# Two graph layers on one core: fp16 products for the whole of layer 1's sum, a mask made by an adding transfer, and a new order

## What is computed

```
h  = x @ W;   e = leaky_relu(h @ a_src + (h @ a_dst)^T)            # 4096 x 4096
valid = adj > 0 and the column's h.sum != 0
att = softmax(where(valid, e, NEG));  att = att where att >= 1e-4, else 0
x1 = layernorm(x + elu(h + (att * valid.sum(axis=1)) @ h))          # layer 0
s  = leaky_relu(x1 @ ks^T), masked by adj > 0, softmax over rows
out = layernorm(x1 + softmax(s) @ ks)                               # layer 1
```

## Time and profile before

| what | value |
|---|---|
| median of 3 runs | 885.51 us (885.41 to 885.6) |
| the profiled execution | 886.26 us, its span 884.4 us |
| TensorE busy | 849.4 us, 96% of the span |
| VectorE busy | 783.3 us, 89% |
| ScalarE busy | 763.8 us, 86% |
| GpSimd busy | 231.0 us, 26% |
| transfers | 43.93 MB counted, mean 50 GB/s |

### The profile page before, as it was taken

One profiled execution on the slowest core, in us unless ns is written; L12 is line 12 of the kernel. 1 busy time (PEld: TensorE's weight loads), 2 busy tenths in 40 slices (PEclk: granted clock), 3 DMA queues, 4 the chain that ended last, 5 costly groups with the idle time before them and its releaser, 6 DMA issues.

```text
span 884.4 us, 17581 instructions
## 1 busy us (share of the span) xinstructions
PE 849.4 (96%) x7111; PEld 732.9 (83%) x7111; DVE 783.3 (89%) x955; ACT 763.8 (86%) x747; POOL 231.0 (26%) x428
## 2 busy tenths in 40 slices
PE   7479999999999999999999999999999999999995
PEld 4376788899888888988888889888888998888885
DVE  1789999999999999999999999999999999998744
ACT  4588988889998888899988888999888889998753
POOL 1431143321223333212233331122333312222200
PEclk9898999999999999999999999999999999999999
DMA  9832222122222211222222112222221122200000
GB/s 236 124 67 50 52 49 41 28 43 55 54 55 54 55 34 30 47 54 55 54 54 54 28 32 53 54 55 54 55 52 24 34 55 54 55 7 7 4 4 10
DMA packets 23408, 43.93 MB, mean 50 GB/s; under 512 B 5024, under 2 KB 18464, under 8 KB 19232
## 3 DMA queue, kind: packets, MB, share of 16 engines
q0 software_dynamic: 7696, 34.34, 21.5%
q1 hardware_dynamic: 15200, 8.39, 3.7%
q10 hardware_dynamic: 432, 0.07, 0.1%
HBM read 75.04 MB, written 2.10 MB: 87 GB/s over the span
## 4 chain that ended last, share of the span: by engine, by line
PE 90%; DVE 3%; DMA 2%; POOL 2%; issue 2%; ACT 1%; POOLq 0%; SPq 0%; DVEq 0%; ACTq 0%
PE bank L336 25%; PE work L234 24%; PE bank L364 10%; PE bank L368 6%; PE work L313 6%; PE work L318 6%; PE work L314 6%; PE bank L365 5%; DMA adj_sb<-adj 1%; DMA att<-x 1%; POOL row L870 0%; POOL edges L879 0%; PE bank L374 0%; DVE att1T L690 0%; ACT att L460 0%
## 5 line engine op out<-in xcount | busy, mean ns | idle before, releaser
L234 PE MATMUL work<-ident,att 128*128 128x128 f32 x2080 | 245.9, 274 | 11.9 <-DMA att<-x 6.0
L234 PEld LDWEIGHTS work<-ident,att 128*128 128x128 f32 x2080 | 232.5, 141 | 19.3 <-issue 9.2
L336 PE MATMUL bank<-h_all,att0T 128*128 128x128 f32 x2048 | 239.1, 275 | 0.0
L336 PEld LDWEIGHTS bank<-h_all,att0T 128*128 128x128 f32 x2048 | 233.7, 192 | 0.0
L500 ACT ACTIVATE att1T<-work 128x1024 f16<-128x1024 f32 (+1 forms) x128 | 125.5, 1048 | 34.7 <-PE work L234 34.7
L640 DVE SCALAR_TENSOR_TENSOR att<-att,cut 128x2048 f32<-128x2048 f32 x64 | 149.7, 2343 | 0.0
L679 DVE CUSTOM_DVE_ANT_0 att<-att,mask 128x2048 f32<-128x2048 f32 x64 | 144.3, 2290 | 5.4 <-ACT att L483 5.4
L364 PE MATMUL bank<-k_parts,att1T 128*128 128x257 f16 x768 | 140.1, 275 | 0.8 <-DVE att1T L690 0.8
L627 DVE CUSTOM_DVE_ANT_0 att<-adj_sb,d_all 128x4096 f32<-128x4096 bf16 x31 | 137.2, 4425 | 1.0
L470 ACT ACTIVATE att<-att,bias 128x2048 f32<-128x2048 f32 x64 | 129.3, 2020 | 7.7 <-POOL bias L873 7.7
L365 PE MATMUL bank<-k_parts,att1T 128*128 128x129 f16 x768 | 134.9, 219 | 0.0
(11 more groups left out here) (98 smaller groups left out, 836.7 us busy)
## 6 DMA issues: line engine op xcount, KB each, us to landing
adj_sb<-adj POOLq DMA_DIRECT2D x32, 1024.0 KB, 8.6
att<-x SPq DMA_DIRECT2D x4, 512.0 KB, 6.6
x_sb<-x SPq DMA_DIRECT2D x32, 64.0 KB, 8.2
out<-x SPq DMA_DIRECT2D x32, 64.0 KB, 1.6
k_parts<-ks POOLq DMA_DIRECT2D x1, 768.0 KB, 20.6
k_rest<-ks SPq DMA_DIRECT2D x1, 512.0 KB, 21.9
w_sb<-W ACTq DMA_DIRECT2D x1, 64.0 KB, 2.9
a_sb<-a ACTq DMA_DIRECT2D x2, 0.5 KB, 4.8
```

What stands on the lines that cost most here:

```text
L234: mm = pe.transpose(work[:, n % SLOTS, b * P:(b + 1) * P], source(c * PER + b), ident[:, :])
L336: mm = pe.matmul(acc0, att0T[:, k * P:(k + 1) * P], h_all[:, k, :], start=(k == 0), stop=(k == BLOCKS - 1))
```

## The change

Seven things change. (1) All four chunks of layer 1's sum are fp16 products; the fp32 branch and its copy of ks (`k_rest`) go, `k_parts` and `k_high` cover all of ks, and VectorE makes a fourth low part. (2) The adjacency is loaded straight into the three `mask` buffers, and `build_mask` works in place, one slot later in relation to the tile. (3) From tile 3 on layer 0's mask is not a minimum on VectorE: SP's queue copies `zero_cols` into `mask_zero`, a transfer from GpSimd's queue adds the adjacency to it, and VectorE turns what is not above zero into the negative number. (4) VectorE's slot: `normalise1` between the two halves of `mask1`, threshold and first cut of the next tile ahead of `mask0`, a low part ahead of `normalise0`, mask building between `normalise0` and `q_low_part`, and two low parts behind that. (5) TensorE interleaves turns and sums of layer 0 and layer 1. (6) ScalarE raises the second half of tile t+1 early in slot t and the first half of tile t+2 late in it. (7) The front: SP waits for adjacency tile 0 before it loads ks, GpSimd for tile 1 before it loads ks as fp16 and then tile 2; the offsets of tiles 0 and 1 and the count of tile 0 are made on VectorE, and TensorE waits for ks only where it turns it.

```diff
-                    if c < SPLIT:
-                        pe.matmul(acc1, high1T[:, part], k_parts[:, k, :], start=(k == 0), stop=False)
-                        mm = pe.matmul(acc1[:, D:], low1T[:, part], k_parts[:, k, D:], start=False,
-                                       stop=(k == BLOCKS - 1))
-                    else:
-                        mm = pe.matmul(acc1[:, D:], att1T[:, part], k_rest[:, k - SPLIT * PER, :], start=False,
-                                       stop=(k == BLOCKS - 1))
+                    pe.matmul(acc1, high1T[:, part], k_parts[:, k, :], start=(k == 0), stop=False)
+                    mm = pe.matmul(acc1[:, D:], low1T[:, part], k_parts[:, k, D:], start=False, stop=(k == BLOCKS - 1))
...
             def slot(t):
                 u, w = t - 1, t - 2
                 score(u, 3)
-                for c in range(CHUNKS):
-                    turn0(t, c)
-                for c in range(3):
-                    sum0(t, c)
+                turn0(t, 0)
+                turn0(t, 1)
+                turn0(t, 2)
+                sum0(t, 0)
+                turn0(t, 3)
+                sum0(t, 1)
+                sum0(t, 2)
                 turn1(u, 0, True)
+                sum0(t, 3)
                 turn1(u, 1, True)
-                sum0(t, 3)
...
             def slot(t):
                 u = t - 1
                 copy0(t, 0)
+                if t + 1 < TILES:
+                    raise0(t + 1, 1)
                 copy0(t, 1)
-                if t + 1 < TILES:
-                    raise0(t + 1, 0)
                 copy0(t, 2)
...
                 elu_exp(t)
-                if t + 1 < TILES:
-                    raise0(t + 1, 1)
-                copy1(u, 2)
-                copy1(u, 3)
-                q_high_part(t)
                 if t + 2 < TILES:
                     bend0(t + 2)
+                copy1(u, 2)
+                q_high_part(t)
+                copy1(u, 3)
+                if t + 2 < TILES:
+                    raise0(t + 2, 0)
...
             def zero_mask(f):
-                dve.wait_ge(mask_built, f + 1)
-                nc.vector.tensor_tensor(adj_sb[f % 2][:, :], mask[f % MASKS][:, :], zero_cols[:, :],
-                                        ALU.min).then_inc(zero_masked, 1)
+                m = mask_zero[f % 2][:, :]
+                if f < EARLY:
+                    dve.wait_ge(mask_built, f + 1)
+                    nc.vector.tensor_tensor(m, mask[f % MASKS][:, :], zero_cols[:, :], ALU.min).then_inc(zero_masked, 1)
+                else:
+                    dve.wait_ge(valid_in[f % 2], 16 * ((f - EARLY) // 2 + 1))
+                    nc.vector.tensor_scalar(m, m, 0.0, -NO_EDGE, ALU.is_le, ALU.mult).then_inc(zero_masked, 1)
...
+                first_offset0(0)
                 zero_mask(1)
                 mask0(1)
+                first_offset0(1)
+                dve.wait_ge(first_bent, QUARTERS)
+                nc.vector.tensor_reduce(absent[0][:, :], first_absent[:, :], AX.X, ALU.add).then_inc(first_counted, 1)
                 threshold0(0)
...
             def slot(t):
                 u, w = t - 1, t - 2
                 mask1(u, 0)
+                if w >= 1:
+                    normalise1(w - 1)
                 mask1(u, 1)
+                if t + 1 < TILES:
+                    threshold0(t + 1)
+                offset1(u)
+                if t + 1 < TILES:
+                    cut(t + 1, 0)
                 if t + 2 < TILES:
-                    build_mask(t + 2)
-                offset1(u)
-                if t + 2 < TILES:
-                    zero_mask(t + 2)
                     mask0(t + 2)
                 residual0(t)
                 low_part1(u, 0)
                 elu(t)
                 if w >= 0:
                     finish1(w)
-                if t + 1 < TILES:
-                    threshold0(t + 1)
+                low_part1(u, 1)
                 normalise0(t)
-                low_part1(u, 1)
+                if EARLY <= t + 1 < TILES:
+                    build_mask(t + 1)
+                q_low_part(t)
                 low_part1(u, 2)
-                q_low_part(t)
-                if t + 1 < TILES:
-                    cut(t + 1, 0)
-                if w >= 1:
-                    normalise1(w - 1)
+                low_part1(u, 3)
                 if t + 1 < TILES:
                     cut(t + 1, 1)
+                if t + 3 < TILES:
+                    zero_mask(t + 3)
...
             def load_adj(f):
-                if f >= 2:
-                    pool.wait_ge(masked0, f - 1)
-                nc.gpsimd.dma_start(adj_sb[f % 2][:, :], adj_rows[f]).then_inc(adj_in[f % 2], 16)
+                if f >= MASKS:
+                    pool.wait_ge(masked1, 2 * (f - MASKS) + 2)
+                nc.gpsimd.dma_start(mask[f % MASKS][:, :], adj_rows[f]).then_inc(adj_in[f % MASKS], 16)
+
+            def add_adj(f):
+                pool.wait_ge(zeros_laid[f % 2], 16 * ((f - EARLY) // 2 + 1))
+                nc.gpsimd.dma_start(mask_zero[f % 2][:, :], adj_rows[f], accum_op=ALU.add,
+                                    max_dma_last_dim=8192).then_inc(valid_in[f % 2], 16)
...
             for t in range(TILES + 2):
+                if 1 <= t < TILES - 2:
+                    load_adj(t + 2)
                 if t + 2 < TILES:
                     offset0(t + 2)
...
                 if t + 4 < TILES:
-                    load_adj(t + 4)
+                    add_adj(t + 4)
```

106 lines of the change are left out of this document (56 added, 50 removed).

## The result

| | before | after |
|---|---|---|
| median | 885.55 us (885.41 to 885.6) | 864.7 us (863.84 to 865.76, 4 runs) |
| ratio after to before | | 0.9766, 95% interval 0.9751 to 0.9782 |
| the profiled execution | 886.26 us, span 884.4 | 863.84 us, span 862.0 |

The kernel is 20.9 us faster by the medians and 22.4 by the two profiled executions, where 21.2 was forecast.

The account below looks back on a forecast made before the run. TensorE was taken as the bound, with 1.3 us of cover over VectorE. -15.7 + 1.5 - 7.5 - 0.9 + 1.4 = -21.2 us from the profiled 886.26 gave 865 us; forecast 861 to 869 (0.62), range 860 to 877.

Parts of the forecast that it names:

- the x1 stall: TensorE's turn of q waits for VectorE's x1 in each slot: 0 to 0.1 us, taken 0.05, times 29: +1.5 us.
- ScalarE's order: First slot: an exponential of 2.0 us goes ahead of two bends TensorE's second turn awaits; +0 to +2.5, taken +1.4 us.
- The fp16 quarter: Layer 1's last quarter on TensorE, fp32 to paired fp16 products: 0.49 us for each of 32 row tiles, -15.7 us.
- Rival A: A much slower adding transfer makes GpSimd's queue set the slot; 1140 us at four times the load's time; chance 0.12.
- X: The adding transfer's engine time in a slot of 6.3 + 3.2 + X: decides from 15 us, slower than before from 16.6.
- The sentence on q's low part: q's low part, now behind mask building, against TensorE's one sum of 1.37 us from turn to score: about 0.1 us spare.
- Rival B: x1 or q's low part comes late to TensorE: a stall of 0.3 us in each slot, 874 us; chance 0.14.
- rival C: GpSimd's coefficient instructions hold up VectorE's mask building, so q's low part is late: 13 us, 878 us; chance 0.07.
- the offsets: Front: offsets of tiles 0 and 1 made on VectorE bring the cut's threshold from 45.19 to 39.8 us: -5.4 us.
- the loads: Front: the first adjacency tile no longer shares the engines with ks, so masking comes 0 to 2.7 us earlier, taken 2.1.
- this pair: Front: the 1.97 us wait for the first coefficient goes, ks's fp16 rest grows by 1.1 us: together -0.9 us.
- the same low stretch: TensorE at a granted 0.52 from 67 to 74 us, assumed the same after; 2.5 us won if it stays high.

Follow-up runs that it names:

- x1's move: The kernel after with x1 (normalise0) ahead of layer 1's second low part and nothing else moved: 863.99 us, ratio 0.9748 to the kernel before.
- the doubled transfer: The kernel after with the adjacency added a second time to each mask buffer from tile 3 on: 921.07 us, ratio 1.0411 to the kernel before.

## Why the prediction was right

The sum came out within 1.2 us of the profiled difference, and most of its terms did too. By the turns of q, in us (the prediction's terms sorted to the same marks and rounded; the x1 stall is in the row of the slots):

| stretch | predicted | measured |
|---|---|---|
| front, to the turn of q of tile 0 | -8.4 | -8.33 |
| to tile 1 (first slot, ScalarE's order) | +1.4 | -0.23 |
| to tile 2 (one shorter quarter) | -0.5 | -0.42 |
| 29 slots, to tile 31 | -12.8 | -13.47 |
| to the end (two shorter quarters) | -1.0 | +0.04 |
| sum | -21.2 | -22.4 |

**The fp16 quarter.** Taken: 1.84 to 1.35 us. Measured: the quarter from 408.27 to 409.62 is 1.35 us, and the slot of TensorE's own work, seen with x1's move, is 24.85 against 25.36, 0.51 less. With the stall of 0.05, just as taken, each slot gains 0.46 us: 13.5 over 29 slots, where these terms make 12.8. The condition on it, that nothing else becomes late, is the one that carried the result. The fp16 products alone gave nothing. With the new order and without the one-input mask they gave 0.30 us a slot (25.36 to 25.06), and with both 0.46. The prediction gave the new order no credit on VectorE's side, where it is worth 0.32 us a slot. That order and mask without the fp16 products would gain nothing in a slot follows from TensorE's slot without a gap before, but no run shows it.

**The mask.** One-input form 1.22 us (taken 1.23). The transfers are hidden: the slot is the same with a plain load. The estimates, 5 and 13 us to landing and 15 to 25 us of the engines per slot, met 5.0, 11.7 and 17.9. Rival A fell, and the doubled transfer shows that its mechanism was rightly described. It was not far off: 0.72 of the engines' time was used, and one more transfer took it to 0.97. Two of its figures do not follow from its own sum: a slot as long as before is not reached from X = 16.6 us, but the whole time of before, 21 us more over 28 slots, at about X = 16.1; and with X = 25 the slot is 6.3 + 3.2 + 25 = 34.5 us, not 34.7.

**The handshakes.** x1's stall was as forecast. The sentence on q's low part had the right place and an incomplete list: it counted from turn to first score and left out that the next two scores wait for the third and fourth low parts. Its terms add up to 1.63 us against 1.37; about 0.1 us to spare comes out only if ScalarE's high part runs beside mask building, as it did. The order chosen by the change is the better one, as moving q's low part cost 14 us. Rival B's price would have been reached by that move.

**GpSimd beside VectorE** (rival C). In the slot mask building stays at 1.22 us and GpSimd is the one held: the second instruction of its coefficient starts 0.05 us behind mask building and takes 1.33 us, where it took 0.29 before. The first line is of before, the second of after:

```profile
424.21 0.29 POOL L882 TENSOR_SCALAR z_sum<-z 128x1 f32<-128x1 f32 x1
```

```profile
409.53 1.33 POOL L907 TENSOR_SCALAR z_sum<-z 128x1 f32<-128x1 f32 x1
```

But the reverse does happen once, in the front, and not with an arithmetic instruction of GpSimd but with the issue of a transfer. With the issue moved away the 0.94 us were gone. The Trainium skill ("SBUF — State Buffer", Who interferes with whom) states that whichever of the two issues first gets the shared pair for the whole instruction. The traces agree but for 0.2 us: the mask, begun second and 1.22 us long by itself, ends 1.0 us behind the issue's end. The price of rival C was real. It did not occur in a slot of the kernel after; in the run with the doubled transfer four of the one-input mask instructions in the slots last 1.33 to 1.53 us, each begun during such an issue.

**The front.** Taken -5.4 for the offsets and -2.1 for the loads; measured by undoing each, 5.7 on the threshold (5.0 in the time) and 2.5 (2.1). The threshold came at 37.43, within the 37 to 38 stated, and the first turns at 40.08. ks's fp16 part takes 4.42 us against 4.5, and the coefficient is awaited 0.19 us against 1.97; residual0 of tile 0 moved by 8.47 us, so this pair gave 0.7 where 0.9 was taken. The term that failed is ScalarE's order in the first slot: +1.4 was taken from a bound of 0 to 2.5, with the clock left as it was, and the step from tile 0's turn of q to tile 1's became 0.23 us shorter. Two things stand against each other in it. From layer 0's second set of turns to tile 1's turn of q it is 17.54 us against 16.88, so the order can have cost up to 0.66 us, and the turns do wait 0.64 us for just the bend that the prediction named. The stretch ahead of it, with the scores, took 8.24 us against 9.12, at a granted 0.66 from 60 to 65 us where the same kind of stretch had 0.52. No run undoes ScalarE's order alone.

**The clock.** I assumed the same low stretch as before. It is not the same one: between 31 and 47 us TensorE was granted 0.64 and 0.73, and the front's 32 turns took 5.49 us. Nor is it the same from one execution to another: with x1's move alone, which changes nothing ahead of them, those two windows have 0.81 and 0.76. It cost little, because other engines set the pace there. What the prediction left out is the tail. Before, the last turns came behind a pause of 2.48 us and ran at the upper level. So they did with the fp16 products alone, behind a pause of 2.96 us (the second line):

```profile
867.82 2.99 PE L234 MATMUL work<-ident,att 128*128 128x128 f32 x24 [2.48 <-ACT att L488]
```

```profile
867.43 2.99 PE L232 MATMUL work<-ident,att 128*128 128x128 f32 x24 [2.96 <-ACT att L476]
```

After, they come behind 2.97 us and take 5.38 us for 32; the window from 842 to 862 has the clock at 0.85. Yet the length of the pause does not settle it. The two changed kernels with the offsets on GpSimd and with GpSimd's issue held back have the same pause of 2.96 us and 24 turns in 2.99 us, and x1's move alone has 32 in 6.57. Why the clock fell in some of these executions and not in others stays open. The price is known: the last quarter's sum starts 17.54 us after the last turn of q before, 17.75 after, and 18.88 with x1's move alone, so 0.21 and 1.34 us. Of the 0.98 us that the sum took for the tail's two quarters, one quarter was never on the path, since TensorE waits for ScalarE behind it (the pause of 2.48 us became 2.97). A miss of +1.0 at the tail, one of -1.6 in the first slot and one of -0.7 over the slots (0.51 us a quarter measured, 0.49 taken, rounding included) partly cancel: to that extent the closeness is luck.

**Against the median.** The forecast of 865 is 0.3 us from the median of 864.7 and 1.2 from the profiled 863.84. As the four runs of the kernel after lie 1.9 us apart, no more should be read into the smaller number.

## What to carry over

When the bounding engine is shortened, ask in the same step what the next one has: here 0.49 us of TensorE was worth nothing until VectorE's full slot of 25.38 us was shortened. A new order of its instructions took off 0.32 us, and it took the one-input form as well to win the last 0.16. In both cases here an engine's cover (1.11 and 0.90 us) was nearer to the slot less its busy time (1.26 and 0.89) than to the waits that the trace names (0.84 and 0.60), and an edit that adds known work measures it. DMA engines that are idle for three quarters of a slot can do arithmetic (here an add with a change of type), once their share after the edit has been reckoned: at 0.72 it cost nothing in a slot, and one transfer more cost 56 us. A difference of 1 us between two kernels whose runs lie 1.9 us apart should be looked for in marks of the trace before it is given a cause.

## What the runs showed of the hardware

- A transfer that converts int32 to bf16 and adds onto 1 MB in SBUF lands in 11.7 us, against 8.6 for the plain converting load of the same rows. In the engines' time it takes some 8.7 us, (0.514 x 862 - 0.215 x 884.4) / 29, from the shares of GpSimd's queue in the two pages. The same reckoning on the run with the plain load (0.429 of 865.9 us) gives 6.3 us for it. A copy of 1 MB within SBUF lands in 5.0 us and takes 2.7, (0.129 x 862 - 0.037 x 884.4) / 29, from SP's queue.
- Issuing a transfer from GpSimd can hold a one-input VectorE instruction on 16-bit data that starts after it: 2.16 us beside an issue of 1.72 that began 0.57 us earlier, 1.64 beside one that began 1.10 us earlier, 1.22 without one.
- One-column instructions of GpSimd that start beside VectorE's long ones last as long as these. The longest, 6.50 us, ends as the second of two two-input instructions of VectorE (43.35 to 49.97 us) does:

```profile
43.58 6.50 POOL L912 TENSOR_SCALAR gate<-z_sum,edges 128x1 f32<-128x1 f32 x1
```

- The granted clock was low after stretches in which TensorE was idle, in the front (4.40 us busy of 9 at 0.64) and, in most executions, in the tail. The same tail with the same pause of 2.96 us had its turns at the upper level in three kernels (24 in 2.99 us) and below it in others (32 in 5.38 and 6.57 us). How much of a clock kept high returns to the time depends on who waits for TensorE: 0.1 us by the trace and 1.2 us by the medians for the front, where other engines set the pace, and 0.2 to 1.3 us for the tail, by how far the clock had fallen.
- In the two slots shown, the VectorE instruction that reads the minimum's result starts 2.32 us behind it, and one that does not read it 2.21 us, beside the minimum's own 2.29 us.
